# Experts in sets of four, and gate weights spread by 0/1 matmuls, in a one-core MetaFormer block

## What is computed

```python
x = x + conv_ref(_ln_c(x), ...)      # 1x1 conv to 192 channels, 5x5 depthwise, grouped 1x1,
                                     # linear attention with 16 heads of 8, projection, batch norm
t = _to_tokens(x)                    # 8 images x 256 tokens x 64 channels
t = t + ffn_ref(_ln_t(t), ...)
# the feed-forward part, xf = 2048 tokens x 64:
gate_logits = xf @ Wg + bg                            # 8 experts
top_w, top_i = jax.lax.top_k(gate_logits, 2)
top_w = jax.nn.softmax(top_w, axis=-1)
w_dense = sum(one_hot(top_i, 8) * top_w[..., None], axis=1)
for e in range(8):
    h = gelu(xf @ W1[e] + b1[e])                      # 64 -> 256
    out = out + w_dense[:, e:e+1] * (h @ W2[e] + b2[e])   # 256 -> 64
```

## Time and profile before

| | us |
|---|---|
| median of 3 runs | 147.06 (146.4 to 148.11) |
| the profiled execution | 146.74 |
| its span, first to last instruction | 145.0 |
| busy: TensorE matmuls / weight loads | 136.1 / 98.3 |
| busy: ScalarE / VectorE / GpSimd | 95.3 / 88.8 / 28.4 |

### The profile page before, as it was taken

The page is one execution under the profiler, slowest core; times in us unless marked ns, Lnnn a source line. Parts: engine busy times, 40 slices in busy tenths (PEclk is TensorE's granted clock), DMA queues, the critical chain, the costliest instruction groups (busy, mean ns, idle before and its releaser), DMA issues.

```text
span 145.0 us, 2718 instructions
## 1 busy us (share of the span) xinstructions
PE 136.1 (94%) x944; PEld 98.3 (68%) x944; DVE 88.8 (61%) x253; ACT 95.3 (66%) x212; POOL 28.4 (20%) x33
## 2 busy tenths in 40 slices
PE   0899899999999999899999999999999999999991
PEld 0368599999998899766675656555656565665650
DVE  0316999999978888854305779955750534421453
ACT  3225799999946844587772676757666775756650
POOL 4199900000000001402201106423110330000000
PEclk9999999999999999999999999999999999999999
DMA  5699000000000000000000000010001000010001
GB/s 148 183 213 223 0 0 7 0 2 5 0 0 0 5 0 0 0 0 5 0 0 0 5 2 2 0 36 0 0 5 36 0 0 5 0 36 0 0 7 36
DMA packets 3655, 3.47 MB, mean 24 GB/s; under 512 B 978, under 2 KB 3258, under 8 KB 3642
## 3 DMA queue, kind: packets, MB, share of 16 engines
q1 hardware_dynamic: 3264, 3.08, 8.3%
q10 hardware_dynamic: 378, 0.22, 0.5%
HBM read 2.78 MB, written 0.52 MB: 23 GB/s over the span
## 4 chain that ended last, share of the span: by engine, by line
PE 92%; DVE 2%; DMA 2%; ACT 1%; issue 1%; DVEq 0%
PE PS L844 54%; PE PS L1034 22%; PE PS L1004 6%; PE PS L926 3%; DMA CST<-in_consts_dram 2%; PE PS L963 2%; PE PS L973 1%; PE PS L932 1%; PE PS L949 1%; PE PS L992 1%; DVE SQ L765 1%; DVE XC L771 1%; DVE BAND L534 1%; ACT KR L397 1%; ACT XS L459 0%
## 5 line engine op out<-in xcount | busy, mean ns | idle before, releaser
L475 ACT ACTIVATE BAND<-PS,B 128x512 f32<-128x512 f32 x64 | 40.5, 687 | 12.0 <-PE PS L844 10.8
L1034 PE MATMUL PS<-BAND,W 128*64 128x256 f32 x256 | 34.4, 391 | 0.0
L765 DVE SCALAR_TENSOR_TENSOR SQ<-PS,B,BAND 128x256 f32<-128x256 f32 x32 | 14.1, 479 | 27.4 <-PE PS L1034 15.2
L844 PE MATMUL PS<-XS,W1H 128*128 128x512 f32 x64 | 28.1, 440 | 0.7 <-ACT XS L459 0.7
L844 PE MATMUL PS<-QP,BAND 128*128 128x120 f32 (+2 forms) x240 | 27.0, 275 | 0.7 <-DVE QP L599 0.7
L844 PEld LDWEIGHTS PS<-QP,BAND 128*128 128x128 f32 x240 | 26.9, 192 | 0.9 <-issue 0.9
L1034 PEld LDWEIGHTS PS<-BAND,W 128*64 128x64 f32 x256 | 15.6, 136 | 15.8 <-issue 10.5
L844 PE MATMUL PS<-XS,W1L 128*128 128x512 f32 x64 | 25.2, 393 | 0.0
L386 ACT ACTIVATE BAND<-RS,PW 128x80 f32<-128x80 f32 x64 | 17.2, 429 | 0.0
L844 PEld LDWEIGHTS PS<-XS,W1H 128*128 128x128 f32 x64 | 12.0, 188 | 6.1 <-issue 3.6
L467 ACT ACTIVATE BAND<-PS 128x512 f32<-128x512 f32 x16 | 9.2, 598 | 10.2 <-PE PS L1004 10.2
(11 more groups left out here) (111 smaller groups left out, 157.0 us busy)
## 6 DMA issues: line engine op xcount, KB each, us to landing
W<-in_w_dram SPq DMA_DIRECT2D x3, 512.0 KB, 6.7
X<-in_x_dram SPq DMA_DIRECT2D x2, 256.0 KB, 3.4
out_dram<-XC SPq DMA_DIRECT2D x4, 128.0 KB, 1.7
VEC<-in_vectors_dram SPq DMA_DIRECT2D x1, 132.0 KB, 3.5
SELF<-in_select_dram ACTq DMA_DIRECT2D x1, 100.8 KB
WQ<-in_w_qkv_dram SPq DMA_DIRECT2D x2, 48.0 KB, 3.6
PW<-in_w_pw_dram SPq DMA_DIRECT2D x1, 96.0 KB, 3.3
CST<-in_consts_dram SPq DMA_DIRECT2D x1, 77.0 KB, 3.5
```

The source lines that it names most:

```text
L475: act.activation(hidden[:, n % HRING, :], PS[:, H_RING[n % 2], :], ACT.Gelu, bias=B1[:, k:k + 1]).then_inc(gelu_done, 1)
L765: dve.scalar_tensor_tensor(out=WY[:, e % 2, :], in0=PS[:, y_bank(s, e), N * (e % 2):N * (e % 2) + N], scalar=B2[:, e:e + 1], in1=WB[:, s % ...
L844: return pe.matmul(PS[0:parts, bank, cols[0]:cols[1]], lhsT, rhs, start=start, stop=stop)
L1034: i = pe.matmul(PS[C * b:C * b + C, y_bank(s, e), N * (e % 2):N * (e % 2) + N], W2[:, KC * e + k, :], hidden[:, (KC * (E * s + e) + k) % H ...
```

## The change

1. **Sets of four.** `second_layer` of experts 0 to 3 (`QUAD`) runs after the first layers of all four, and so on. In the last pair all eight second layers come at the end. For that the ring `hidden` has 16 blocks, 12 of them in the free tensor `MS`; the results of second layers have two banks (2 and 3) in turn; the GELU blocks have two banks for the first four blocks, then four (0, 1, 6, 7).
2. **Spreading by matmul.** The gate weights of a pair are split on VectorE in a high and a low fp32r half (`WDS`), transposed once (two transposes with 32 rows out, inside `tokens`), and copied by ScalarE into `WT`. `weights(s, ep)` is now two fp32r matmuls of a constant 0/1 matrix `PICK` with `WT`, 256 columns each. `WIDE` and its copies on GpSimd and VectorE are gone. ScalarE makes `PICK` (1024 elements a partition) once, among the convolution's bands.
3. **Gate logits in two parts** of two pairs each, with the tokens on partitions from the start: `XS` is the stationary operand, the gate weights' high and low half (`WGS`, 16 columns) the moving one, eight small matmuls a part. `copy_gates` and `turn_gates` are gone. Part 0 comes right behind `attt(3)`, and its softmax ahead of `scale(3)` on VectorE; GpSimd does its power ahead of the last `deviation`.

The diff, cut to its core:

```diff
-        HRING = 4
-        hidden = late(HRING, PT)
+        HRING, IN_MS = 16, 12
+        hidden_more = late(HRING - IN_MS, PT)
...
-        SOFTMAX_PARTS = slice(0, TILES), slice(TILES, PAIRS * TILES)
+        PARTS = 2
+        OF_PART = PAIRS // PARTS
+        SOFTMAX_PARTS = slice(0, OF_PART * TILES), slice(OF_PART * TILES, PAIRS * TILES)
...
-        Y_BANK0 = 0
-        H_RING = (6, 7)
-        MISC = (4, 5)
-        MISC_USES = 1 + E // 2
-
-        MISC_SLOT = (6, 7, 9, 9, 10, 11, 13, 14, 15, 16, 18, 19, 20, 21, 21, 23, 24, 24, 26, 29)
+        H_FEW, H_MANY, FEW = (6, 7), (0, 1, 6, 7), 4
+        Y_BANKS, LAST_Y_BANK = (2, 3), 6
+        MISC = (5, 4)
+        GATE_BANKS = 1, 4
+        MISC_GATES = (3,)
+        QUAD = 4
...
+        def h_bank(n):
+
+            return H_FEW[n % 2] if n < FEW else H_MANY[n % 4]
+
+        def h_before(n):
+
+            return max((m for m in range(n) if h_bank(m) == h_bank(n)), default=None)
...
+            return LAST_Y_BANK if s == PAIRS - 1 and e == E - 1 else Y_BANKS[e // 2 % 2]
...
+            pool.memset(WT[:, :, :].bitcast(F32), 0.0).then_inc(pads_set, 1)
+            pool.wait_ge(pads_set, 6)
...
-            pool.wait_ge(wdn_ready, 4)
-            pool.wait_ge(wide_ready, E // 2)
-            for s in range(1, PAIRS):
-                for ep in range(E // 2):
-                    pool.wait_ge(misc_ready, MISC_USES * (s - 1) + 2 + ep)
-                    pool.tensor_copy(*widened(s, ep)).then_inc(wide_ready, 1)
+            deviation(0)
+            deviation(1)
+            deviation(2)
+            exponential(0)
+            deviation(3)
+            exponential(1)
...
-                act.activation(WGH[:, :], WG[:, :], ACT.Copy).then_inc(w_high, 1)
+                act.activation(WGS[:, 0, :], WG[:, :], ACT.Copy).then_inc(w_high, 1)
+                act.wait_ge(cst_in, 16)
+                act.activation(PICK[:, :, :, :].rearrange("p e b c -> p (e b) c"),
+                               CST[:, C_ROWS:C_ROWS + 2 * E].unsqueeze(2).broadcast_to([128, 2 * E, C]),
+                               ACT.Copy).then_inc(pick_set, 1)
...
+            def read_tokens(s):
+
+                n = misc_use(s, 0)
+                act.wait_ge(misc_ready, uses_before(n) + 1)
+                if s >= 2:
+                    act.wait_ge(misc_ready, uses_before(misc_use(s - 1, 0)))
+                act.activation(WT[0:4 * E, s % 2, :], PS[0:4 * E, MISC[n % 2], N:2 * N], ACT.Copy).then_inc(wt_read, 1)
+                act.activation(outs[:, s, :], PS[:, MISC[n % 2], 0:N], ACT.Copy).then_inc(misc_read[n % 2], 1)
...
             square_xc(2)
             copy_attt(3)
             gelu(0, 2)
+            gelu(0, 3)
+            high(2)
             square_xc(3)
-            high(2)
-            gelu(0, 3)
+            gelu(0, 4)
             copy_xs(2)
+            gelu(0, 5)
+            gelu(0, 6)
             high(3)
-            gelu(0, 4)
             copy_xs(3)
-            for s in range(PAIRS):
-                for e in range(5 if s == 0 else 0, E):
-                    gelu(s, e)
-                    for n in range(MISC_USES * PAIRS):
-                        if MISC_SLOT[n] == E * s + e:
-                            read_misc(n)
+            read_tokens(0)
+            gelu(0, 7)
...
+                dve.wait_ge(gate_ready, part + 1)
+                logits = LOGITS[:, tiles, :]
+                of = PS[:, GATE_BANKS[part], 0:2 * E * count].rearrange("p (t k e) -> p k t e", k=2, e=E)
+                link(dve.tensor_tensor(logits, of[:, 0], VEC[:, 4 * C:4 * C + E].unsqueeze(1)
+                                       .broadcast_to([128, count, E]), ALU.add))
+                dve.tensor_tensor(logits, of[:, 1], logits, ALU.add).then_inc(gate_read, 1)
+                dve.wait_ge(gate_read, part + 1)
...
+                link(dve.tensor_copy(parts[:, 0].bitcast(F32R), whole))
+                dve.tensor_tensor(parts[:, 1].bitcast(F32R), whole, parts[:, 0], ALU.subtract).then_inc(wds_ready, 1)
...
             attend(3)
+            read_gates(0)
             variance(2)
+            gaps(0)
             scale(2)
             residual(3)
             low(2)
             variance(3)
+            places(0)
+            softmax(0)
             scale(3)
             low(3)
-            copy_gates()
-            read_gates()
-            top2(0)
-            softmax(0)
-            widen(0)
-            widen(1)
-            widen(2)
             dve.wait_ge(b2_in, 32)
-            for s in range(PAIRS):
-                for ep in range(E // 2):
-                    combine(s, ep)
-                    if s == 0 and ep == 0:
-                        top2(1)
-                        widen(3)
-                    if s == 0 and ep == 1:
-                        softmax(1)
+            combine(0, 0)
+            read_gates(1)
+            combine(0, 1)
+            gaps(1)
+            places(1)
+            combine(0, 2)
+            softmax(1)
+            for n in range(3, PAIRS * E // 2):
+                combine(*divmod(n, E // 2))
...
-            def gate():
-
-                for s in range(PAIRS):
+            def gate(part):
+
+                pairs = range(OF_PART * part, OF_PART * (part + 1))
+                for s in pairs:
                     pe.wait_ge(a_read[s], A_XT)
-                for s in range(PAIRS):
-                    for k, w in enumerate((WGH, WGL)):
-                        i = pe.matmul(PS[:, MISC[0], :], w[:, GZ - GM * s:GZ - GM * s + 128], XS[:, s, :],
-                                      start=s == k == 0, stop=s == PAIRS - 1 and k == 1)
+                pe.wait_ge(w_low, 3)
+                if part == 0:
+                    pe.wait_ge(b_read[1], B_PROJ)
+                for n in MISC_GATES if part == 1 else ():
+                    pe.wait_ge(misc_read[n % 2], reads_before(n))
+                for s in pairs:
+                    for t in range(TILES):
+                        at = 2 * E * (TILES * (s - pairs[0]) + t)
+                        i = mm(GATE_BANKS[part], (at, at + 2 * E), XS[:, s, 128 * t:128 * t + 128],
+                               WGS[:, :, :].rearrange("p k e -> p (k e)"), True, True)
                 i.then_inc(gate_ready, 1)
 
-            def turn_gates():
-                pe.wait_ge(gates_copied, 1)
-                pe.wait_ge(b_read[PAIRS - 1], B_PROJ)
-                for t in range(TILES):
-                    i = pe.transpose(PS[:, MISC[1], 128 * t:128 * t + 128], GATES[:, 128 * t:128 * t + 128], IDT)
-                i.then_inc(gates_turned, 1)
+            def wait_misc(n):
+
+                if n in (MISC_GATES[0] + 1, MISC_GATES[-1] + 1, MISC_GATES[-1] + 2) and n not in MISC_GATES:
+                    pe.wait_ge(gate_read, 2)
+                if n >= 2:
+                    pe.wait_ge(misc_read[n % 2], reads_before(n))
+                else:
+                    pe.wait_ge(b_read[PAIRS - 1], B_PROJ)
+                    pe.wait_ge(a_read[PAIRS - 1], A_XT)
 
             def tokens(s):
 
-                n = MISC_USES * s
-                if n >= 2:
-                    pe.wait_ge(misc_read[n % 2], n // 2)
-                else:
-                    pe.wait_ge(gate_read, 1)
+                n = misc_use(s, 0)
+                wait_misc(n)
+                pe.wait_ge(wds_ready, s // OF_PART + 1)
+                for half in range(2):
+                    pe.transpose(PS[0:4 * E, MISC[n % 2], N + 128 * half:N + 128 * half + 128],
+                                 WDS[:, s, half].rearrange("p k b e -> p (k b e)"), IDT)
...
+                wait_misc(n)
+                pe.wait_ge(wt_read, s + 1)
+                pe.wait_ge(pick_set, 1)
...
+                    i = mm(MISC[n % 2], (N * e, N * e + N), PICK[:, 2 * ep + e].rearrange("p b c -> p (b c)"),
+                           WT[:, s % 2, :], True, True)
...
-                    if n >= 2:
-                        pe.wait_ge(gelu_done, n - 1)
+                    if h_bank(n) == GATE_BANKS[0] and n < 2 * FEW:
+                        pe.wait_ge(gate_read, 1)
+                    if h_before(n) is not None:
+                        pe.wait_ge(gelu_done, h_before(n) + 1)
+                    elif h_bank(n) == 0:
+                        pe.wait_ge(a_read[1], A_XT)
                     for m, w in enumerate((W1H, W1L)):
-                        i = mm(H_RING[n % 2], (0, PT), w[:, 128 * k:128 * k + 128], XS[:, s, :], m == 0, m == 1)
+                        i = mm(h_bank(n), (0, PT), w[:, 128 * k:128 * k + 128], XS[:, s, :], m == 0, m == 1)
                     i.then_inc(h_ready, 1)
...
+                if E * s + e >= 4:
+                    pe.wait_ge(y_read, E * s + 2 * (e // 2) - 2)
+                else:
+                    pe.wait_ge(a_read[2], A_XT)
+                    pe.wait_ge(b_read[2], B_PROJ)
...
             first_layer(0, 1)
             attt(3)
-            second_layer(0, 0)
+            gate(0)
             first_layer(0, 2)
+            first_layer(0, 3)
```

(74 more changed lines are left out.)

165 lines of the change are left out of this document (88 added, 77 removed).

## The result

The changed kernel took 140.32 us (median of 4 runs, 139.89 to 140.62), the kernel before 147.31 us in the same session: ratio 0.953, 95% interval 0.948 to 0.958. The forecast was 140.2 us. The sum behind it was right in its main term, and smaller errors of both signs cancelled.

A forecast was written before the change was run, and what follows sets the result against it. TensorE's queue was taken to bound the feed-forward part. The terms summed to -6.9 us, bringing the span from 145.0 to 138.1, the execution to 139.8 and the median to 140.2 us; range 137.3 to 143.8.

The forecast's parts named there:

- item 1: TensorE: runs of second layers fall from 30 to 7, -8.3 us; calls of one kind side by side lose +0.4.
- item 2: TensorE: 16 spreads at 0.37 us become pairs of 256-column fp32r matmuls at 0.28, -1.4 us.
- 3 tokens: TensorE: two more transposes in each `tokens`, 4 x 0.2, +0.9 us with the one that loses its neighbour.
- 4 gate logits: TensorE: gate matmuls and their turning, 2.03 + 0.41, give way to 16 matmuls with 16 columns, 1.9: -0.5 us.
- 5a: TensorE: GELU block 5 waits for VectorE to read the logits out of bank 1, +0.3 us.
- 5b: TensorE: the first `tokens` waits for the copy of XS of pair 3, +0.85 us.
- Item 6: VectorE's end: after one run of eight second layers it has both last experts to do, 1.91 us against 0.93: +0.85.
- A: Spreads: 256-column fp32r matmuls run at plain fp32 pace, 0.96 a pair, 10.9 us dearer: 151 us; 2 in 100.
- C: Second layers: each costs 1.02 us even in a run, +4.0, 144.2 us; 6 in 100.
- B: Front-loaded stretch: ScalarE gets late, so `xt(3)` and the copy behind it come late, +1.5, 141.7 us; 15 in 100.
- D: TensorE's granted clock falls from 2.4 to 1.2 GHz; a fall of 10 us is +5, 145 us; 2 in 100.
- E: The seven runs of second layers are cut apart by waits, above all for `y_read`; no room seen beyond B and C.

The follow-up runs named there:

- experiment 3: Changed kernel, but from pair 2 on each second layer singly behind a first layer, only the last four in a run; 143.92 us, ratio 0.979 to the kernel before.
- second pair of profiles: Both kernels run and profiled again, unchanged: the kernel before 146.93 us, ratio 1.000; the changed kernel 139.55 us, ratio 0.950.
- experiment 4: Changed kernel, but GELU blocks have two PSUM banks all along instead of four from the fifth block on; 151.88 us, ratio 1.033 to the kernel before.
- experiment 10: Changed kernel plus one memset with an unused result at the start of VectorE's list; 139.29 us in one execution.

## Why the prediction was right

The price list held, and with it the main term. By the prediction's items, in us:

| item | forecast | measured | from |
|---|---|---|---|
| 1 fewer runs, 23 | -8.3 | -7.9 | 0.34 a run, experiment 3 |
| 1 first layers and spreads side by side | +0.4 | 0 | no matmul behind another call of its kind starts late |
| 2 spreads | -1.4 | -2.2 | 16 x (0.235 - 0.37) |
| 3 tokens | +0.9 | +1.2 | 8.46 - 8.01 = 0.45 for one, a set of four with and without |
| 4 gate logits | -0.5 | -0.6 | 0.90 + 0.81 + 2 x 0.08 for 2.44 |
| 5a block 5 waits for the logits' reading | +0.3 | +0.2 | 0.41 - 0.23 |
| 5b first `tokens` behind the copy of XS | +0.85 | +1.0 | 78.02 - 77.03 |
| sum on TensorE | -7.75 | -8.3 | of -8.79 in the table above |
| 6 tail | +0.85 | +1.3 | 2.40 - 1.10 |
| 7 `PICK` and the convolution | 0 | 0 | 27.0 long, as before |
| start | 0 | +1.0 | chance; -0.25 in the second pair of profiles |

The items give -8.3 of the -8.8 seen; the half microsecond left belongs to none that I can name. The prices are read to 0.01 us and taken up to 23 times, which alone can make some 0.4. Of the items, experiments 3 and 4 test the first. The others are read from rows of the two profiles; no run takes the spreads or the gate part back.

**Where a size was off.** The term that mattered most is item 2. I had half of a 512-column matmul's spacing, 0.117, and added "a little for the waits in front". The waits cost nothing, 0.235 a pair is twice that half, and the 0.045 on each of sixteen makes 0.7. The same caution stood in item 1's 0.4. By the formula of the Trainium skill (TensorE: Matmul & The Clock Gate, "Back-to-back issue gap") a pair is estimated at 0.22; the trace shows 0.24, and the rows decide. Item 6 missed the hole of 0.41 in VectorE's list, which the end of the kernel before does not have, and of which experiment 10 says that it is a matter of the instruction's position: 0.3 of the 0.45 that was missing. Another 0.13 is a slip: the item's own figures, 1.91 and 0.93, give +0.98, not +0.85. The low end of the range does not follow from its reason either: items 2 and 5 at their cheap ends take 0.8 and 1.15 off, which gives 138.2, not 137.3.

**Where it was luck.** That the median came within 0.1 us of the forecast is luck. TensorE saved 1.0 more than forecast, the tail cost 0.45 more, and a start 1.0 later in the profile more than made up for the difference. The second series, 139.55, is what the measured middle columns give: 146.93 - 7.5 = 139.4.

**The rivals.** A and C fell by the rows: 256 columns in 0.117, second layers 0.87 apart, and singles at 1.0 only where they stand alone (experiment 3). B did not come: `xt(3)` starts at 76.62 straight behind the second layers, so that the half microsecond to spare sufficed. How much depends on TensorE running ahead of ScalarE shows in experiment 4, where the two take turns. D did not come: 1.00 through every stretch from 17 to 134 us, with both holes in it, and TensorE cycling through four banks. What the Trainium skill (TensorE: Matmul & The Clock Gate, "A second HAM failure mode: psum-queue depth-cycling") describes did not come here. E fell: no wait within a run of second layers.

**What the profile was to show.** Sets of four take 105.52 - 97.06 = 8.46 with tokens and 8.01 without, the latter under my 8.2; spreads, second layers and both holes are as said; VectorE ends 2.4 behind TensorE, not 1.9.

## What to carry to other kernels

Read start-to-start distances in a steady stretch, not listed durations, and make a price of every kind of call and of every change between kinds: here going from first to second layers and back cost 0.34 to 0.36 us a time, and grouping calls saved 8 of 80 us. Grouping needs depth in buffers: with two PSUM banks in place of four the same order was 3% slower than the kernel before, since the engine that follows can then no longer lag and catch up. A hole in a chain is only worth removing with the one behind it: moving one call gained nothing, moving two, and dropping a wait between them, gained 0.6 in the profile.
